# Writing out all 68 slots of a pipelined encoder layer in place of a loop over four slots, with constant waits

## The reference

```python
q, k, v = heads(x @ wq + bq), heads(x @ wk + bk), heads(x @ wv + bv)   # 8 heads of 48
scores = einsum('bhqd,bhkd->bhqk', q, k) * 48 ** -0.5 + adj[:, None]
ctx = einsum('bhij,bhjd->bhid', softmax(scores), v)
x1 = rmsnorm(x + (ctx @ wo + bo), alpha1, gamma1)
y = rmsnorm(x1 + (silu(x1 @ w1 + b1) @ w2 + b2), alpha2, gamma2)       # w1: 384 x 1536
out = layernorm(x + y)                                                  # eps 1e-5
```

## Time and profile before

| | |
|---|---|
| median of three runs | 3330.17 us (3328.28 to 3331.51) |
| profiled execution: its time, first to last instruction (span) | 3330.1 us |
| TensorE matmuls busy | 3073.1 us, 92% |
| VectorE busy | 2062.4 us, 62% |
| ScalarE busy | 1460.2 us, 44% |
| GpSimd busy | 701.6 us, 21% |
| DMA | 171.86 MB, mean 52 GB/s |
| instructions fetched | 232 packets, 3.80 MB |

### The profile page before, as it was taken

The page is one execution under the profiler, slowest core; times in us unless marked ns, Lnnn a source line. Parts: engine busy times, 40 slices in busy tenths (PEclk is TensorE's granted clock), DMA queues, the critical chain, the costliest instruction groups (busy, mean ns, idle before and its releaser), DMA issues.

```text
span 3330.1 us, 64046 instructions
## 1 busy us (share of the span) xinstructions
PE 3073.1 (92%) x25216; PEld 2960.5 (89%) x25216; DVE 2062.4 (62%) x3621; ACT 1460.2 (44%) x4262; POOL 701.6 (21%) x968
## 2 busy tenths in 40 slices
PE   5899999999999999999999999999999999999998
PEld 5889889899898898998998988988988989889897
DVE  4666665666665656656666666566666665666665
ACT  4444444444444444444444444444444444444433
POOL 0122221221221212212212212122122121221221
PEclk7899999999999999999999999999999999999999
DMA  5212112112121121121111211211212112112110
GB/s 140 70 31 61 45 47 61 36 57 61 31 61 50 42 61 42 50 61 36 56 57 35 61 48 44 61 36 56 61 31 61 48 44 61 41 51 61 36 45 25
DMA packets 155434, 171.86 MB, mean 52 GB/s; under 512 B 18608, under 2 KB 155184, under 8 KB 155184
## 3 DMA queue, kind: packets, MB, share of 16 engines
q1 hardware_dynamic: 155184, 167.91, 17.1%
HBM read 92.35 MB, written 25.17 MB: 35 GB/s over the span
## 4 chain that ended last, share of the span: by engine, by line
PE 77%; DVE 11%; ACT 7%; issue 5%; SPq 0%; DMA 0%; POOL 0%; POOLq 0%; DVEq 0%; ACTq 0%
PE ps_work L429 43%; PE ps_rows L514 17%; PE ps_rows L429 6%; ACT probs L656 5%; PE ps_probsT L458 4%; DVE h L850 3%; PE ps_ctx L477 2%; DVE neg_max L783 2%; DVE probs L779 2%; PE ps_ctx L481 2%; DVE x1T L828 2%; ACT h_raw L706 1%; DVE probs L792 1%; PE ps_work L552 1%; PE ps_scores L443 1%
## 5 line engine op out<-in xcount | busy, mean ns | idle before, releaser
L514 PE MATMUL ps_rows<-w_s,h 128*128 128x384 f32 x4608 | 915.7, 361 | 1.5 <-DVE y L861 1.5
L514 PEld LDWEIGHTS ps_rows<-w_s,h 128*128 128x128 f32 x4608 | 877.3, 206 | 10.4 <-DVE y L861 2.1
L429 PE MATMUL ps_work<-x1T,w_s 128*128 128x256 f32 x6912 | 844.7, 283 | 0.2 <-ACT h_raw L706 0.2
L429 PEld LDWEIGHTS ps_work<-x1T,w_s 128*128 128x128 f32 x6912 | 833.3, 188 | 0.5 <-ACT h_raw L706 0.4
L656 ACT ACTIVATE probs<-probs,neg_max 128x128 f32<-128x128 f32 x1024 | 396.2, 389 | 387.1 <-DVE neg_max L783 387.1
L706 ACT ACTIVATE h_raw<-ps_work,b_col 128x256 f32<-128x256 f32 x768 | 322.0, 471 | 429.6 <-PE ps_work L429 419.6
L850 DVE CAST h<-h_raw 128x512 fp32r<-128x512 f32 x384 | 264.0, 688 | 287.9 <-ACT h_raw L706 287.9
L852 DVE TENSOR_TENSOR h<-h_raw,h 128x512 fp32r<-128x512 f32 x384 | 361.9, 942 | 13.2
L388 POOL TENSOR_SCALAR mean_sq<-sum_sq 128x1 f32<-128x1 f32 x256 | 48.7, 190 | 1514.0 <-ACT squares L663 1514.0
L458 PE MATMUL ps_probsT<-ident,probs 128*128 128x128 f32 x1024 | 158.2, 303 | 182.6 <-DVE probs L792 182.6
L458 PEld LDWEIGHTS ps_probsT<-ident,probs 128*128 128x128 f32 x1024 | 123.9, 154 | 207.5 <-DVE probs L792 194.0
(11 more groups left out here) (74 smaller groups left out, 3700.8 us busy)
## 6 DMA issues: line engine op xcount, KB each, us to landing
qk<-qk_flat SPq DMA_DIRECT2D x384, 96.0 KB, 2.4
x_in<-in_x SPq DMA_DIRECT2D x64, 384.0 KB, 3.3
x_res<-in_x SPq DMA_DIRECT2D x64, 384.0 KB, 3.9
x_last<-in_x SPq DMA_DIRECT2D x64, 384.0 KB, 3.2
out<-y SPq DMA_DIRECT2D x64, 384.0 KB, 2.5
bias<-in_adj SPq DMA_DIRECT2D x64, 128.0 KB, 3.7
qk<-qk_flat SPq DMA_DIRECT2D x128, 64.0 KB, 2.1
stage<-in_L_gnn_w SPq DMA_DIRECT2D x24, 192.0 KB, 3.2
```

Of the source, the lines that this page charges most:

```text
L429: mm = pe.matmul(ps_out, stationary(sta), moving(mov), start=(i == 0), stop=(i == n - 1))
L514: mm = pe.matmul(ps_rows[:, 0:d], h[:, sta, m, b * P:(b + 1) * P], w2_s[:, mov, m, :], start=(m == 0 and i == 0), stop=(m == fc - 1 and i ...
```

## The change

The engine loop is gone. `run_slots` calls `slot_program` for all 68 slots with a Python integer, so every wait is on a constant and every DRAM address is fixed. `static` goes with it, as do the branches that chose between the two forms. The order of the work on every engine is that of before.

```diff
-UNROLL = 4
-    loop_from, loop_to = -(-(LAG_FF2 + 2) // UNROLL) * UNROLL, groups
-        def static(g):
-            return isinstance(g, int)
         def live(g):
-            return not static(g) or 0 <= g < groups
+            return 0 <= g < groups
-        def run_slots(engine, slot):
-            for t in range(loop_from):
+        def run_slots(slot):
+            for t in range(slots):
                 slot(t, t % 2)
-            with engine.Fori(loop_from // UNROLL, loop_to // UNROLL) as turn:
-                for i in range(UNROLL):
-                    slot(turn * UNROLL + i, i % 2)
-            for t in range(loop_to, slots):
-                slot(t, t % 2)
         def group_rows(ap, g):
-            if static(g):
-                return ap[g * PAIR:(g + 1) * PAIR].rearrange("b n e -> n b e")
-            return ap[bass.ds(g * PAIR, PAIR)].rearrange("b n e -> n b e")
+            return ap[g * PAIR:(g + 1) * PAIR].rearrange("b n e -> n b e")
...
                 if b == 0:
-                    if static(g):
-                        dve.wait_ge(bias_loaded[parity], 16 * (g // 2 + 1))
-                    else:
-                        dve.wait_ge(bias_loaded[parity], (g - parity) * 8 + 16)
+                    dve.wait_ge(bias_loaded[parity], 16 * (g // 2 + 1))
...
-            run_slots(pe, slot_program)
+            run_slots(slot_program)
```

More of the change, by code:

```diff
@@ L63, in build_layer @@
     slots = groups + LAG_FF2
-    loop_from, loop_to = -(-(LAG_FF2 + 2) // UNROLL) * UNROLL, groups
     assert nodes == P and kd * P == d and HEADS == 8 and 2 * rest == TILE and dh <= HALF
-    assert UNROLL % 2 == 0 and loop_to % UNROLL == 0
     ctx = ExitStack()
@@ L256, in weights_due @@
         def weights_due(t, point):
-            return schedule.get((t, point), ()) if static(t) else ()
+            return schedule.get((t, point), ())
         n_vectors = 10
@@ L327, in slot_program @@
             def slot_program(t, parity):
-                if live(t) and not (static(t) and t == 0):
+                if live(t) and not (t == 0):
                     load_x(t)
@@ L362, in slot_program @@
                         sp.dma_start(qk[to:to + n, :, pair, :], qk_flat[p0:p0 + n, :, c, :]).then_inc(qk_moved, 16)
[L363 to L367, removed]
+                for n in weights_due(t + 1, 0):
+                    load_weights(n)
+            run_slots(slot_program)
             sp.wait_ge(y_stored, 16 * groups)
@@ L417, in slot_program @@
                                        ALU.add).then_inc(x1_b2_ready, 1)
-            run_slots(pool, slot_program)
+            run_slots(slot_program)
         @block.tensor
@@ L522, in project_qk @@
                                             ((wk_s, 1), (wk_s, 2)))):
-                    if static(g) and g == 0 and n < 2:
+                    if g == 0 and n < 2:
                         pe.wait_ge(weight_split, (n + 1) * kd)
@@ L539, in project_v @@
             def project_v(g):
-                if static(g) and g == 0:
+                if g == 0:
                     pe.wait_ge(weight_split, proj_units)
@@ L607, in slot_program @@
                 if live(g_ff2):
-                    if static(t) and t == LAG_FF2:
+                    if t == LAG_FF2:
                         pe.wait_ge(weight_split, len(units))
@@ L621, in slot_program @@
                 if live(g_attn):
-                    if static(t) and t == LAG_ATTN:
+                    if t == LAG_ATTN:
                         pe.wait_ge(weight_split, out_units)
@@ L634, in slot_program @@
                 if live(g_ff1):
-                    if static(t) and t == LAG_FF1:
+                    if t == LAG_FF1:
                         pe.wait_ge(weight_split, up_units)
@@ L712, in slot_program @@
                 g_proj, g_attn, g_ff1, g_ff2 = t - LAG_PROJ, t - LAG_ATTN, t - LAG_FF1, t - LAG_FF2
-                if static(t) and t == 1:
+                if t == 1:
                     act.wait_ge(vectors_loaded, 16 * n_vectors)
@@ L751, in slot_program @@
                     act.preload_act_table(ACT.Exp)
-            run_slots(act, slot_program)
+            run_slots(slot_program)
         @block.vector
@@ L925, in slot_program @@
                 weights_lo(t, 5)
-                if static(t) and t == 0:
+                if t == 0:
                     scale_query_bias()
@@ L935, in slot_program @@
                     transposed_lo(g_attn, 1, ps_ctx, x1T_hi, x1T, x1T_lo)
-            run_slots(dve, slot_program)
+            run_slots(slot_program)
 _INS = ["x", "adj"] + ["L0_gnn_" + n for n in (
```

## The result

| | before | after |
|---|---|---|
| first comparison, median | 3329.23 us (3324.46 to 3331.51, 4 runs) | 3343.64 us (3343.11 to 3344.40, 4 runs) |
| ratio, 95% interval | | 1.0043 [1.0029, 1.0057] |
| repeated, median | 3334.6 us (3324.44 to 3340.94, 16 runs) | 3341.72 us (3339.97 to 3342.16, 12 runs) |
| ratio, 95% interval | | 1.0023 [1.0014, 1.0032] |

Writing the slots out makes the kernel slower, by 14.4 us in the first comparison and by 7.1 us in the repeated one. The new kernel varies by 1 to 2 us from run to run, the loop by 7 to 17.

A forecast was written before the change was run, and what follows sets the result against it. The prediction took TensorE's work and its standstills, chiefly the wait for the softmax multiply, as the bound. It added 9.1 us for the 56 slots and 0 for other parts to 3330.1, giving 3339.2 us, range 3332 to 3343.

The forecast's parts named there:

- The bound: TensorE's work plus its standstills: 182.6 us at the probability transposes, 30.2 us of "issue" at the scores.
- The stall is absorbed: At 13 back edges, the 30.2 us removed return as TensorE's wait for the softmax multiply and slowed matmuls.
- TensorE's busy time: Sign expected in the new profile: TensorE's busy time rises by 5 to 10 us.
- the drain: The 143.68 us after the loop: no term in the sum, up to 1.5 us more in the range.
- the instruction queue: Sign expected in the new profile: the instruction queue carries more than 3.80 MB.
- The slots: The loop's 56 slots, 2857.45 us, take 2866.2 or 2867.0 written out: +8.8 or +9.5, taken as +9.1 us.
- Constant waits, streamed code, other branches: 0: Register waits made constant, code fetched in sequence, and branches on engines other than TensorE: each worth 0.
- the base: Starting time of the sum: 3330.1 us, taken as the profiled execution's time before the change.
- (c): Rival: streamed code stalls ScalarE or VectorE between L779 and L792, giving 3371 us; chance 0.04.
- rival (b): No visible change, 3330 to 3336 us: written-out slots drift against the clock and some escape its fall; chance 0.18.
- Rival (a): The back-edge stall is net cost that written-out code gets back: 3299.9 us; chance 0.05.

The follow-up runs named there:

- loop_of_two: The kernel before with its loop over two slots in place of four: 3343.33 us, ratio to before 1.0039.
- gpsimd_adds_moved: The written-out kernel with GpSimd's three wide adds moved away from the slot's boundary: 3083.04 us, ratio 0.9256.
- wait_every_fourth: The written-out kernel with an added TensorE wait ahead of the scores at the 13 places of the old back edges: 3342.46 us, ratio 1.0034.
- written_again: The changed kernel unaltered, run again with many runs of the kernel before beside it: median 3341.72 us, ratio 1.0023.
- loop_adds_moved: The kernel before, its loop over four slots kept, with GpSimd's wide adds moved off the slot's boundary: 3122.57 us, against 3083.04 written out.

## Why the prediction was right or wrong

**The bound, right.** The wait at the probability transposes is what matters, and the 13 "issue" waits were the branch on TensorE. loop_of_two, whose branch is 0.208 us, shows the second; gpsimd_adds_moved the first.

**The stall is absorbed, right.** The row of waits rose by 42.0 us; "about 13 x 3.42 = 44" was forecast. The count rose from 56 to 66, not to 69: the prediction took the wait as gone behind every edge, and behind three of the 13 a short one was left. The slot where the first edge was has the wait and the slow second product back. That a pair of slots gains about 1 us and the next pays it back is what wait_every_fourth shows with equal stalls, up to slot 57: 0 in the sum.

**Two signs that failed.** TensorE's busy time was to rise by 5 to 10 us; it rose from 3073.1 to 3073.9. It fell by 2.0 in the 56 slots and rose by 2.6 in the drain: the slow stretches that the written-out slots have behind the wait, the loop had elsewhere, in the first down product behind an edge and in the slot that pays back. What the change costs is standing time. And the instruction queue was to carry more than 3.80 MB: the one that was meant carries 3.28, and only with the second are there more, 4.02 against 3.95.

**The slots, right but 0.7 low.** 56 slots written out: 2867.25 us measured, 2866.2 and 2867.0 were the two estimates and the mean was taken. +9.8 in place of +9.1. The longer sample, seven slots, was the better one.

**Constant waits, streamed code, other branches: 0, right.** Slots without an edge are 51.20 us in both forms. Only at the head of a turn, with a long wait put there, did the loop start 0.18 us later.

**What failed: terms of the sum.** The forecast was 3330.1 + 9.1. The mechanism and the sign were right; the base was 1.8 us too low, the drain was put at 0 and measured +2.56, and the slots were 0.7 too low. The drain: the text let the slow stretches there move and gave them "up to 1.5" in the range only; in the profiled execution they cost +2.56 (in that of written_again 1.5), since slots 65 to 67 have a mean clock of 0.91, where they had 0.96 before. The base: "the profiled execution's time" was taken as its span, 3330.1. In every listed run the time is 1.7 to 1.9 us above the span (3344.40 us with a span of 3342.6), so that the profiled execution of before stands for about 3331.9, an estimate. With these, 3331.9 + 9.8 + 2.6 = 3344.3, against 3344.40 for the profiled execution after. That the median moved by 14.4 and not by 12.5 comes from the kernel before: its profiled execution was 2.7 us above the median that it was compared with, 3329.23. A single profile of a kernel that varies by 7 us was read as if it were exact, and the upper end of the range had no room for that. The prediction's own working put that end at 3343.5 (3330.1 + 12.0 + 1.5 is 3343.6), and its range then stopped at 3343. The shares behind it do not add up exactly either: 0.70 less a tenth of it, with (c), is 0.67 and not 0.70.

**The drift of rival (b).** It was given 0.18. In the profiled execution after it did not happen; in that of written_again it did once (slot 12), and the time was 3341.72 in the median, 2 us lower. So both are ways of this kernel, and neither makes up for the loop. The prediction's sentence that a slot passes the wait without a fall "only where edges have disturbed the rhythm" is wrong by that slot, which has no edge ahead of it; slot 9 of loop_of_two, without a stall, is another, 49.60 us at 1.00.

**Rival (a), the 30 us back,** fell, as the Trainium skill's sentence on full unrolling (Runtime: NRT & Kernel Launch, "Instruction fetch mechanics") does for this kernel: with the wait in place written-out code is slower. loop_adds_moved shows where the sentence holds: once the wait is gone, a stall is worth 3.04 us each. The other half of the page's rule, that a target not held forces a fetch, agrees with 3.70 against 0.208 us at four and two slots per turn, and with 3.80 against 0.41 MB in the instruction queue.

**What was missed.** The prediction named VectorE's queue as the start of the softmax chain and did not ask why L779 started 5.4 us into the slot. Two ops in front of it took five and three times as long as the same ops elsewhere.

## What to carry to other kernels

A stall that the chain of waits shows is worth its length only if no later wait on the same engine absorbs it: look in the same slot or turn for a wait that is missing where the stall stands. If there is one, remove that wait first, by what holds its releaser up; here three adds on GpSimd moved away from the slot's boundary gave 8.2%, and only behind that did the back edge become worth 1.3%. When two instructions of one form have durations several times apart, ask what the other engines do at that moment.

## What the runs showed of the hardware that was not expected

- A back edge over four slots took TensorE 3.70 us, with 3.80 MB in the instruction queue; over two slots it took 0.208 us, with 0.41 MB. The other engines took 0.045 to 0.056 us with four.
- An added wait of 2.3 us in every slot made the kernel 2% faster (3265.85 us). A slot of 51.20 us with one standstill of 3.43 us has a stretch at the lower clock nearly each time (mean granted clock 0.97), and its second down product takes 8.14 us in place of 6.49. With a stall of 2.29 us at both ends a slot takes 50.0 us with such a stretch and 49.56 us without (clock 1.00), and 22 of 56 are without.
- Wide adds on GpSimd stretch VectorE's copy of 128x512 fp32 from 0.43 to 2.01 us and its difference from 0.69 to 2.22 us, while its op that reads PSUM beside them keeps its 1.21 us.
- The written-out kernel repeats to 1.3 us in 4 runs and 2.2 in 12; the loop over four slots varies by 7 to 17 us. With 13 stalls put into written-out code it varies by 6.9 us in 6 runs (even ones) and 8.7 in 10 (of two lengths).
